# Attention with relation bias: key logits kept in SBUF, a ring of four query tiles, clamped sums moved from VectorE to GpSimd

## The reference, cut to what matters

```python
attn_scores = jnp.einsum('bihd,bjhd->bhij', q, k) / scale
logits = li[:, :, None, :] + lj[:, None, :, :] + rel_b      # three per pair (i, j)
relation_probs = jax.nn.softmax(logits, axis=-1)
bias = jnp.einsum('bijk,hk->bhij', relation_probs, logical_bias)
attn_scores = attn_scores + gate * bias
attn_weights = jax.nn.softmax(attn_scores, axis=-1)
out = jnp.einsum('bhij,bjhd->bihd', attn_weights, v)
```

## Time and profile before

| | us |
|---|---|
| median of 3 runs | 5028.67 |
| lowest, highest run | 5019.67, 5031.66 |
| profiled execution, its own time | 5015.02 |
| its span, first to last instruction | 5013.2 |
| attention chunks 0 to 31, first to last exponential of the scores | 336.9 to 4182.1 |
| granted TensorE clock, mean over the span | 0.898 |

### The profile page before, as it was taken

How to read it: one execution, slowest core, us unless ns; L and a number is a source line. 1 busy time by engine, 2 the same in 40 slices (tenths; PEclk the granted TensorE clock), 3 DMA queues, 4 the chain that set the end, 5 groups by cost and what they waited for, 6 DMA issues and landing times. The chain is left out here.

```text
span 5013.2 us, 248173 instructions
## 1 busy us (share of the span) xinstructions
PE 3750.1 (75%) x106896; PEld 2787.7 (56%) x106896; DVE 3755.9 (75%) x6310; ACT 3323.6 (66%) x3946; POOL 2024.0 (40%) x1816
## 2 busy tenths in 40 slices
PE   7457777777777777777777778777777776289992
PEld 4225555555555555555555555555555555257772
DVE  4498887888888888888888788888888843167773
ACT  2128777777777777877787777877777883034440
POOL 0114444444444444444444444444444442433335
PEclk8669999999999999999999899999999998589996
DMA  6213333333333333333333333333333335244443
GB/s 107 67 38 95 97 98 95 95 97 98 97 94 93 96 96 97 100 95 94 98 97 95 94 95 95 100 98 98 95 97 98 96 103 190 77 145 146 155 138 113
DMA packets 405084, 510.32 MB, mean 102 GB/s; under 512 B 109296, under 2 KB 343152, under 8 KB 400016
## 3 DMA queue, kind: packets, MB, share of 16 engines
q1 hardware_dynamic: 394800, 476.50, 31.2%
q0 software_dynamic: 6144, 16.79, 1.1%
q10 hardware_dynamic: 3040, 0.98, 0.1%
HBM read 237.99 MB, written 46.40 MB: 57 GB/s over the span
## 5 line engine op out<-in xcount | busy, mean ns | idle before, releaser
L732 DVE TENSOR_REDUCE b_mxp<-b_mx 128x1 f32<-128x512 f32 x4096 | 2579.7, 680 | 531.3 <-PE b_mx L848 509.4
L704 ACT ACTIVATE b_pr<-b_sc 128x1024 f32<-128x1024 f32 x2048 | 1982.4, 1020 | 893.0 <-PE b_sc L829 874.1
L871 PE MATMUL b_acc<-b_pr,vp 128*32 128x128 f32 x32768 | 1207.3, 288 | 25.2 <-issue 23.2
L848 PE MATMUL b_mx<-kst,b_qx 64*128 64x512 f16 x4096 | 849.8, 410 | 415.5 <-DVE b_mxp L732 399.1
L815 PE MATMUL b_sc<-b_cm,b_rst 64*128 64x64 f16 x32768 | 789.9, 196 | 494.8 <-DMA b_rst<-b_rhi 343.0
L627 POOL TENSOR_TENSOR b_ex<-b_ex 128x512 f32<-128x512 f32 x512 | 676.2, 1321 | 990.0 <-ACT b_ex L682 987.3
L815 PEld LDWEIGHTS b_sc<-b_cm,b_rst 64*128 64x128 f16 x32768 | 679.7, 98 | 690.0 <-issue 437.7
L871 PEld LDWEIGHTS b_acc<-b_pr,vp 128*32 128x32 f32 x32768 | 892.9, 115 | 304.9 <-issue 288.8
L724 DVE TENSOR_SCALAR b_dl<-b_dj,b_const 128x512 f32<-128x512 f32 x1024 | 693.5, 679 | 193.7 <-DMA b_dj<-key_logits 191.9
L637 POOL CAST b_rhi<-b_ex 128x512 f16<-128x512 f32 x512 | 325.6, 636 | 1089.4 <-ACT b_ex L691 977.8
L829 PE MATMUL b_sc<-b_qm,kst 64*128 64x64 f16 x32768 | 716.4, 195 | 37.1 <-issue 34.4
(11 more groups left out here) (144 smaller groups left out, 1627.8 us busy)
## 6 DMA issues: line engine op xcount, KB each, us to landing
b_dj<-key_logits SPq DMA_DIRECT2D x256, 512.0 KB
b_rst<-b_rhi SPq DMA_DIRECT2D x1024, 128.0 KB
b_rst<-b_rlo SPq DMA_DIRECT2D x512, 128.0 KB
c_w1r<-in_L_ffn_W_dram SPq DMA_DIRECT2D x23, 1024.0 KB, 4.8
c_w2r<-in_L_ffn_W_dram SPq DMA_DIRECT2D x23, 1024.0 KB, 4.8
expert_tokens<-c_zeros SPq DMA_DIRECT2D x23, 512.0 KB, 6.8
c_xb<-expert_tokens SPq DMA_DIRECT2D x23, 512.0 KB
expert_results<-c_y SPq DMA_DIRECT2D x23, 512.0 KB, 2.9
```

What stands on the lines that cost most here:

```text
L704: nc.scalar.activation(pr[:, jt % 2, half, :], sc[:, half].rearrange("p a b -> p (a b)"), ACT.Exp).then_inc(s["p_ready"], 1)
L732: nc.vector.tensor_reduce(mxp[:, head, part:part + 1], mx[:, (bank + ab) % MX_RING, :], AX.X, ALU.max).then_inc(s["mx_used"], 1)
L848: pe.matmul(mx[:, (bank + ab) % MX_RING, :], qx[rows, par, pair, :], kst[rows, pair, j0:j0 + 512], start=True, stop=True).then_inc(s["mx_r ...
L871: ins = pe.matmul(acc[32 * (h % 4):32 * (h % 4) + 32, h // 4, :], vp[:, jt, VW * h:VW * h + 32], pr[:, jt % 2, h % 2].rearrange("p (a h i) ...
```

## The change

- The key logits `dj` of all eight units are loaded once, before the first chunk, and stay. The loads at the end of each unit and the wait for `d_ready` ahead of them are gone.
- The queries of a chunk are loaded once, into one slot of a ring of four (`qt`), by two DMAs of 128 KB each in unit 2, two chunks ahead; `qm` and `qx` are gone, and products and maxima read the same tile. For this, the parts of the keys are laid out high, high, low, low, and those of the queries high, low, high, low.
- The clamped sums run on POOL (`pool_d`), two of 128x512 per group, between the sum of the exponentials and the cast, two groups ahead.
- In unit 6 the row maxima go out after the first step and come back after the third, where both stood behind the fourth.
- The loop body has eight chunks, three turns, and eight chunks follow it.

```diff
-R_AHEAD, D_AHEAD = 4, 3
-CLAMP_SLOT, ACC_SLOT = 1, 0
-UNROLL, LOOPS = 10, 3
+R_AHEAD, D_AHEAD = 4, 2
+ACC_SLOT = 0
+UNROLL, LOOPS = 8, 3
+QR = 4
...
-                            for row, part in ((0, 0), (16, 1), (32, 0), (48, 1)):
+                            for row, part in ((0, 0), (16, 0), (32, 1), (48, 1)):
...
-        dj = sb("dj", [P, 2, 2, JU])
+        dj = sb("dj", [P, UNITS, 2, JU])
-        qm = sb("qm", [P, 2, PAIRS, P], F16)
-        qx = sb("qx", [P, 2, PAIRS, P], F16)
+        qt = sb("qt", [P, QR, PAIRS, P], F16)
...
+        def sp_q(sp, x, par, slot4):
             for ab in range(2):
+                sp.dma_start(qt[64 * ab:64 * ab + 64, slot4].rearrange("r q t -> r (q t)"),
+                             q_dram[bass.ds(x, 1), ab].rearrange("o a r q t -> o (a r) (q t)").broadcast_to(
+                                 [2, 2 * HD, PAIRS * P])).then_inc(s[f"q_in{par}"], 16)
...
-            sp_q(sp, 1, 1, qx, "qx_in1")
-            sp_q(sp, 0, 0, qm, "q_in")
+            sp_q(sp, 1, 1, 1)
+            for u in range(2, UNITS):
+                sp_dj(sp, u)
...
-                    if u == M_UNIT and not last:
-                        sp_m_out(sp, c + 1)
-                        sp_m_in(sp, c + 1, 1 - par)
-                    if u + 4 < UNITS or not last:
-                        sp.wait_ge(s["d_ready"], 32 * c + 4 * u + 12)
-                        waited(sp)
-                        sp_dj(sp, (u + 4) % UNITS)
+                        if u == M_UNIT and step == 0 and not last:
+                            sp_m_out(sp, c + 1)
+                        if u == M_UNIT and step == 2 and not last:
+                            sp_m_in(sp, c + 1, 1 - par)
                     if u == 1:
                         sp_att(sp, c)
-                    if u == 2 and not last:
-                        sp_q(sp, c + 1, 1 - par, qm, "q_in")
-                    if u == 3 and more:
-                        sp.wait_ge(s["c_made"], 2 * c + 2)
-                        waited(sp)
-                        sp_q(sp, c + 2, par, qx, f"qx_in{par}")
+                    if u == 2 and more:
+                        sp_q(sp, c + 2, par, (slot4 + 2) % QR)
...
+        def pool_d(pool, x, par, nth, g):
+            u, side = g // 2, g % 2
+            if g == 0:
+                pool.wait_ge(s[f"const_in{par}"], 80 * nth)
+            if isinstance(x, int) and x == 0:
+                pool.wait_ge(s[f"dj_in{min(u // 2, 1)}"], 32 if u < 2 else 16 * (UNITS - 2))
+            if not (isinstance(x, int) and x == 0 and g < 2):
+                pool.wait_ge(s["e_ready"], 16 * x + g - 1)
+                pool.sem_inc(s["pool_waited"], 1)
+            for n in range(2):
+                nc.gpsimd.tensor_scalar(dl[:, side, n], dj[:, u, n], const[:, par, side, n:n + 1], EXP_MAX, ALU.add,
+                                        ALU.min).then_inc(s["d_ready"], 1)
...
                     if g < 2 * UNITS:
                         pool_sum(pool, c, g)
                     elif not last:
                         pool_sum(pool, c + 1, g - 2 * UNITS)
+                    ahead = g + D_AHEAD
+                    if ahead < 2 * UNITS:
+                        pool_d(pool, c, par, nth, ahead)
+                    elif not last:
+                        pool_d(pool, c + 1, 1 - par, nth + par, ahead - 2 * UNITS)
...
-                        if slot == CLAMP_SLOT:
-                            g, k = R_AHEAD + (jt + D_AHEAD) // 2, (jt + D_AHEAD) % 2
-                            if g < 2 * UNITS:
-                                dve_d(dve, c, par, nth, g, k)
-                            elif not last:
-                                dve_d(dve, c + 1, 1 - par, nth + par, g - 2 * UNITS, k)
```

More of the change, by code:

```diff
@@ L557, in _ @@
         def _(sp):
-            sp_q(sp, 0, 0, qx, "qx_in0")
+            sp_q(sp, 0, 0, 0)
             sp.wait_ge(s["cval_zeroed"], 1)
@@ L575, in _, with chunk @@
             sp_m_in(sp, 0, 0)
-            def chunk(c, par, nth, last):
+            def chunk(c, par, nth, last, slot4):
                 more = not last and not (isinstance(c, int) and c + 2 >= NT)
@@ L712, in _ @@
             in_chunks(act, chunk)
-        def dve_d(dve, x, par, nth, g, n):
-            u, side = g // 2, g % 2
-            if g == 0 and n == 0:
-                dve.wait_ge(s[f"const_in{par}"], 80 * nth)
-            if side == 0 and n == 0:
-                dve.wait_ge(s[f"dj_in{u % 2}"], 16 * (UNITS // 2 * x + u // 2 + 1))
-            if n == 0 and not (isinstance(x, int) and x == 0 and g < 2):
-                dve.wait_ge(s["e_ready"], 16 * x + g - 1)
-            nc.vector.tensor_scalar(dl[:, side, n], dj[:, u % 2, n], const[:, par, side, n:n + 1], EXP_MAX, ALU.add,
-                                    ALU.min).then_inc(s["d_ready"], 1)
         def dve_pair(dve, x, n, bank):
@@ L765, in _ @@
             for n in range(PAIRN):
-                if n % 2 == 0 and n < 2 * R_AHEAD:
-                    for k in range(2):
-                        dve_d(dve, 0, 0, 1, n // 2, k)
                 dve_pair(dve, 0, n, 2 * n)
@@ L772, in _, with chunk @@
                 dve_pair(dve, 1, n, 2 * PAIRN + 2 * n)
-            for n in range(D_AHEAD):
-                dve_d(dve, 0, 0, 1, R_AHEAD + n // 2, n % 2)
-            def chunk(c, par, nth, last):
+            def chunk(c, par, nth, last, slot4):
                 more = not last and not (isinstance(c, int) and c + 2 >= NT)
@@ L829, in pe_products @@
                         ins = pe.matmul(sc[:, ab, side, pair * IS:pair * IS + IS], kst[rows, pair, jt * P:jt * P + P],
-                                        qm[rows, par, pair, side * IS:side * IS + IS], start=False,
+                                        qt[rows, slot4, pair, side * IS:side * IS + IS], start=False,
                                         stop=(pair == PAIRS - 1), skip_group_check=True)
@@ L833, in pe_products, with pe_scores, pe_pair, pe_step_pair @@
                             ins.then_inc(s["scores_ready"], 1)
[L835 removed]
+        def pe_scores(pe, c, par, slot4, jt):
             pe_relation(pe, c, par, jt, 0)
             pe_relation(pe, c, par, jt, 1).then_inc(s["relation_done"], 1)
[L839 to L841 removed]
+            pe_products(pe, c, slot4, jt)
+        def pe_pair(pe, x, par, nth, slot4, n, bank):
             pair, j0 = n // MXU, n % MXU * 512
             if n == 0:
[L845 removed]
+                pe.wait_ge(s[f"q_in{par}"], 32 * nth)
             for ab in range(2):
                 rows = slice(64 * ab, 64 * ab + 64)
[L848 removed]
+                pe.matmul(mx[:, (bank + ab) % MX_RING, :], qt[rows, slot4, pair, :], kst[rows, pair, j0:j0 + 512],
                           start=True, stop=True).then_inc(s["mx_ready"], 1)
[L851 removed]
+        def pe_step_pair(pe, c, par, nth, slot4, jt, slot, last, more):
             n = 2 * jt + slot + AHEAD
```

52 lines of the change are left out of this document (19 added, 33 removed).

## The result

The changed kernel takes 4776.44 us (median of 4 runs, 4773.54 to 4781.96), the kernel before in the same session 5024.17 (5013.83 to 5031.66). The ratio is 0.951, 95% interval 0.9489 to 0.9531: a gain of 248 us. The forecast of 4380 us was a gain 2.6 times as large, and the measured time lies outside the range of 4270 to 4640. The profiled execution has a span of 4780.2 us.

What follows compares the result with a forecast made beforehand. Bound: the ACT-PE loop, 94.6 of 120.9 us per chunk, plus waits for `rst` loads and DVE. New chunk 94.6 + 4.3 + 2.0 = 100.9; savings 620 + 1 + 26 = 647 from 5015.0 give 4368, forecast 4380, range 4270 to 4640.

Steps and rivals of the forecast that it cites:

- Clamps on POOL: Clamped sums moved to POOL: 0.64 us each, bounds 0.6 and 1.33; POOL at 73.3 us per chunk, nothing reaching PE.
- Rival D: POOL becomes the loop once a clamp there exceeds 1.51 us; at 1.585 the kernel takes 4706 us; chance 0.06.
- Rival E: Slower than before, with POOL's clamp above 2.13 us; at 2.5 the kernel takes 5369 us; chance 0.03.
- Key logits resident: Eight loads per chunk removed: PE's 10.7 us waiting for `rst` and DVE's 3.2 for key logits go.
- Before chunk 0: At the start, DVE's wait for first key logits and eight clamps go: minus 26 us, bounds 0 and minus 29.
- rival B: Only the DMA stalls go; ordinary tiles keep small waits as DVE's cover is too thin: 4571 us; chance 0.19.
- Query ring: Query loads, eight DMAs of 64 KB made two of 128 KB: 0 taken, or one stall of 4.8 us per chunk.
- Rival C: The query load on two DMA engines still stalls a unit, 4.8 us each chunk: 4529 us; chance 0.09.
- Clamps off DVE: 21.6 us of DVE work per chunk go, leaving 87.0 of maxima; PE's 9.2 us of waits for DVE taken as gone.
- Row maxima earlier: SP's wait for the maxima's trip to DRAM moves ahead: between minus 2 and plus 2 us, taken as 0.
- What stays: Per chunk, PE's idle by issue, 4.3 us, all on the path, plus 2.0 at chunk's end for the accumulator.
- Loop turns: Program loop's back edges, two before and two after the change: nothing.

Runs made afterwards that it cites:

- e5: The changed kernel with six forms of the 128x512 operation on POOL, one per group in turn, to read durations; 4514.89 us (1 run).
- e3: The kernel before with one edit: key logits of all units stay in SBUF, loaded once; 4563.86 us, ratio 0.9067 to before.
- e4: The kernel before with one edit: the clamped sums on POOL, key-logit loads kept; 5223.18 us, ratio 1.0389 to before.
- e1: The changed kernel with its clamped sums back on DVE, two per group; 4547.82 us, ratio 0.9042 to before.
- e7: The changed kernel with add-multiply in place of add-minimum on POOL, so not the wanted values; 4393.41 us, ratio 0.8739 to before.
- e2: The changed kernel with one clamped sum of each group on POOL and the other on DVE; 4410.58 us, ratio 0.8768 to before.
- e8: The kernel before with each key-logit load issued as two of 64 partitions, source beginning with the broadcast of 64; 4660.43 us, ratio 0.9266 to before.

## Why the prediction was wrong

The sign was right, the size was not. **The step that failed is "Clamps on POOL"**, as the prediction put it: "It has one tensor input, like the cast, so I take 0.64, bounds 0.6 and 1.33." It measured 1.996, and the same form 2.00 in e5. With it fell what stood behind it, "nothing reaches PE": POOL's sum per chunk was not 73.3 us but 112.4, more than the forecast chunk of 100.9, so POOL set the pace and ACT and PE waited for its sum of exponentials. The 13.2 us between the measured chunk of 114.1 and 100.9, 31 times over, are 409 us, and 4380 + 409 = 4789 is the measured time to within 13. The bounds were wrong too, since I took the dearest POOL row at hand, the two-input sum, for an upper end. The number of tensor inputs isn't what sets the price: the row of a cast says nothing on an add with a minimum.

Rival D had the mechanism, its place and its threshold: above 1.51 us per clamp POOL is the path. With the measured price its formula gives 52.7 + 32 x 1.996 = 116.6 plus its handovers; measured are 113.8 in a plain chunk, as the other POOL operations became shorter (1.324 to 1.270 us for the sum) once DVE no longer did clamps beside them, and the handovers vanish in an engine that never waits. Both signs named for D show: ACT's wait for the sum above, and SP's wait for `lo_ready`, 728.9 us in 2000. I gave D 0.06, and 4706 for a price of 1.585. Rival E, slower than before, lay only 0.13 us per clamp further on.

Point by point, otherwise:

- *Key logits resident*: 13.9 us per chunk were forecast. Measured from before to e3: 120.9 to 106.6, 14.3 per chunk.
- *Before chunk 0*: the first score exponential of the change is at 309.0 us, where about 310 was forecast. It is at 309.2 in e4, which keeps the loads, and at 345.1 in e3, later than the 336.9 of before, with DVE still clamping. So the 26 us come from taking the clamps off DVE, and rival B was wrong to add them to a gain from the DMA stalls alone.
- *Query ring*: nothing, as taken; e1 and e3 can't be told apart. Rival C fell: while the query load of the change is alone (1600.3 to 1602.5 us) it holds two engines of sixteen, and in e7, where POOL doesn't cover a stall, PE waits 9.2 us in 2000 for `rst`, 0.5 per chunk in place of C's 4.8:

```profile
q1 hardware_dynamic: 44, 0.09, 13.3%
```

- *Clamps off DVE*: DVE at 84.0 per chunk (87 forecast). The 87.0, and the 21.6 for the clamps, add up durations that overlap in the trace. 128 maxima of 0.686 are 87.8 us in the change too, yet DVE is busy for 84.0 in all, and the clamps' going took 15.6, or 0.49 each. The 96 to 99 expected of e2 has the same fault. With POOL's price put right (e7), PE's wait for DVE is 12.7 us in 2000, 0.6 per chunk against 9.2 before, so rival B fell. In e1, where DVE keeps them, it stays at 8.9. On the path the relief is 5.0 us (106.6 in e3 to 101.6 in e7), near the 20.0 - 13.9 = 6.1 of the sum.
- *Row maxima earlier*: SP's wait for their trip is 0.6 us in 2000 against 79.0, and it waits 61.5 us for DVE's maxima in its place, as foreseen. On the path this is nothing that e1 and e3 can tell, as taken.
- *What stays*: issue was taken as 4.3 per chunk; e7 has 40.2 + 32.4 + 15.0 + 4.5 = 92.1 us in 2000, 4.7 per chunk. At the chunk's end 2.0 were taken for the accumulator: on average over chunks 11 to 25 of e7 the first three tiles of a chunk take 3.51 us each, 1.7 in all over the 2.96 of the loop.
- *Loop turns*: a turn isn't free, it costs 4.4 us in the change. But there are two of them as before, so nothing is left of it in the difference, as taken.
- *The Trainium skill's word against the move* ("GPSIMD Engine Reference", section 4.1) was right that this work is cheaper on VectorE and, by the rows, wrong on the price: it has one-input elementwise work at roughly line rate, and the same clamp takes 0.478 us undisturbed on DVE and 1.996 on POOL, 4.2 times as long. Even so, half of the clamps on POOL is the best of these kernels (e2).
- *The clock* has no term in the sum. PE is busy 93.8 us per chunk before and 89.3 in e3, which does the same work at a granted clock of 1.00 in place of 0.93. How much of these 4.5 us lay on the path no run tells.

## What to carry to other kernels

An operation that the trace doesn't hold has to be measured in its own form, the pair of operations included, before it gets a price. A row of another form on the same engine is no bound. Ask at which price each engine becomes the loop before you choose a price, and give that case weight by how near it lies, not by how unlikely the price looks: here the threshold was 1.51 and one engine would carry 32 instructions of unknown cost per chunk.

When work can sit on either of two engines and would fill either, split it (e2). And look at what a DMA's slowest source dimension is: a broadcast that begins with 2 held two engines for some 76 of 121 us (estimate from rows 8) and delayed loads that had nothing to do with it.

## What the runs showed of the hardware

- On GpSimd a 128x512 f32 tensor-scalar operation takes 0.62 us for add-multiply or multiply-add with constants and 0.69 with a per-partition column, but 1.49 to 1.50 for one operation alone (multiply, minimum) and 1.92 to 2.01 for the other pairs tried (add-minimum, add-add, maximum-minimum, maximum-multiply, multiply-minimum).
- The same key-logit load runs at 55 GB/s on two DMA engines and at 266 GB/s on sixteen when its source begins with the broadcast of 64 (e8).
- GpSimd and VectorE slow each other. In e1 a clamp on VectorE takes 0.478 us on average when POOL is idle meanwhile and 0.782 when POOL works for at least 0.1 us of it, and POOL's sum of exponentials takes 1.324 to 1.338 us with both clamps on VectorE (before, e1, e3, e8) and 1.269 to 1.277 with none (the change, e4, e7).
- Without the long stalls PE's granted clock in the chunks is 0.99 to 1.00 (the change, e1, e2, e3, e7, e8) in place of 0.93 and 0.91 (e4). In the kernel before, a stretch at 1.2 GHz followed a wait of PE's own. PE stood for 4.41 us until 2213.05, waiting for `rst`:

```profile
2211.00:2213.00 2.00, 0.00 (x0) 0.00 (x0) 0.00 (x0) 0.00 (x0) 1.19 (x2) 0.50 0.14 51
2213.00:2215.00 2.00, 1.95 (x66) 1.79 (x66) 0.00 (x0) 0.03 (x1) 0.00 (x0) 0.50 0.13 53
2219.00:2221.00 2.00, 1.82 (x66) 1.39 (x67) 2.00 (x5) 2.00 (x3) 0.20 (x1) 1.00 0.42 129
```
